# One block of sliding-window attention: the order of TensorE's products by array tile, and a mask product over 64 rows

## The chip, the cores and the metric

The kernel runs on one core of one Trainium2 chip. Its time is the device time of one execution in microseconds (us). The profile names the engines PE (TensorE's matmuls), PEld (TensorE's weight loads), DVE (VectorE), ACT (ScalarE), POOL (GpSimd) and SP (SyncE).

## The reference, cut to what matters

Two deformable convolutions on 8 images of 64 channels and 32x32 pixels come first. Then each image is 1024 tokens of 64 channels, and goes through sliding-window attention (8 heads, each query sees the 32 last keys) and a layer of experts. The change touches the attention alone:

```
q = (x @ Wq.T).reshape(b, t, h, e) / scale
kk = (xp @ Wk.T).reshape(b, tp, h, e) / scale
v = (xp @ Wv.T).reshape(b, tp, h, e)
idx = jnp.arange(t)[:, None] + jnp.arange(k)[None, :]
kw = kk[:, idx]
vw = v[:, idx]
dot = jnp.einsum('bthe,btkhe->bthk', q, kw)
attn = jax.nn.softmax(dot, axis=-1)
out = jnp.einsum('bthk,btkhe->bthe', attn, vw)
out = out.reshape(b, t, h * e)
return out @ Wu.T + bu
```

## The kernel before, in words

The attention works on blocks of 128 tokens of a pair of images: 32 blocks (ALL_BLOCKS). One image of the pair lies in partitions 0 to 63, the other in 64 to 127. Each engine has its own program, written out by hand, and the engines meet through counting semaphores; nothing else sets the order. Each program has a short lead-in, then a loop over 7 rounds of 4 blocks (`body(i)`, `BODY = 4`), and the last 4 blocks written out. Inside round b of the body several blocks are in flight: queries of block b+4, scores of b+3, keys of b+2, turned probabilities of b+1, values of b.

TensorE does these for a block, each product in float32 (two MATMUL records for one product) but for the mask:

- queries (L821): 8 products of 64 rows by 128 columns of the array, 128 columns of data each, the two images in the two halves of the rows. ScalarE copies the results out (L950).
- scores: first the mask, 2 products in float16 of 32 rows by 128 columns with 512 columns of data (L834), which write the mask into both score banks, then 16 products of 64 rows by 128 columns with 64 columns of data (L844). VectorE takes the maximum (L1007) and subtracts it (L1009, semaphore `shifted`), ScalarE takes the exponential (L956), VectorE sums (L1015) and inverts (L1017), GpSimd multiplies (L1085, `probs_ready`).
- turned probabilities (L869): 4 transposes of 128x128 for each image half ("image" 0 and 1), copied out by ScalarE (L962, `pt_ready`).
- turned keys (L857): 2 transposes of 128x128, copied out by VectorE (L1023, `xw_ready`).
- values (L888): 8 products of 64 rows by 64 columns for image 0, and 8 for image 1. ScalarE copies each result out (L968, `z_ready`).
- projection (L903): 8 products of 128 rows by 64 columns; VectorE adds the result to the tokens (L1033, `added`).

Ahead of the values of an image stand three waits (`before_values`). VectorE has raised `z_ready` to 1 before the first block, and every copy L968 adds 1:

```
pe.wait_ge(at.pt_ready, (i * BODY + b) * 2 + image + 1)
if image == 0:
    pe.wait_ge(at.xw_ready, i * BODY + b + 1)
pe.wait_ge(at.z_ready, (i * BODY + b) * 2 + image + 1)
```

So the values of image 1 of block b wait for a count of 2b + 2: 1 from VectorE, 2b copies of earlier blocks, and the copy of image 0 of block b itself.

TensorE's order in a round is queries (b+4), values of image 0 (b), turn of image 0 (b+1), mask and scores (b+3), values of image 1 (b), turn of image 1 (b+1), turned keys (b+2), projection (b). In two places the waits before the values stand one product early (`carry`), ahead of the last product of the queries and of the scores.

Of the kernel before, what the change touches and what calls it, by code (L numbers as in the profile page):

```python
# [15 lines left out]
NIMG, C, H, W = 8, 64, 32, 32  # L16
PAIRS = NIMG // 2
P = 128
# [655 lines left out]
HG = 2  # L674
H4 = HEADS // HG
# [120 lines left out]

TURN_AHEAD, KEYS_AHEAD, SCORES_AHEAD, QUERIES_AHEAD = 1, 2, 3, 4
ALL_BLOCKS = PAIRS * BLOCKS
# [11 lines left out]
def attention_pe(nc, pe, m, at):  # L810
    def queries(i, b, carry=None):

        pe.wait_ge(at.windows_ready, i * BODY + b + 1)
        if b:
            pe.wait_ge(at.g_ready, (i * BODY + b) * 2)
        for h in range(H4):
            for image in range(2):
                rows = slice(C * image, C * image + C)
                if carry is not None and (h, image) == (H4 - 1, 1):
                    carry()  # L820
                last = nc.tensor.matmul(m.ps[:, image, h * P:(h + 1) * P], at.a_heads[rows, h, :],  # L821
                                        at.window[rows, b % 4, WINDOW:SPAN], start=True, stop=True)
                if h == H4 - 1:
                    last.then_inc(at.g_in_psum, 1)

    def scores(i, b, carry=None):

        pe.wait_ge(at.g_ready, (i * BODY + b) * 2 + 2)
        pe.wait_ge(at.swapped_ready, (i * BODY + b) * 2 + 2)
        if b:  # L830
            pe.wait_ge(at.shifted, i * BODY + b)
        for hg in range(HG):
            rows = slice(TQ * hg, TQ * hg + TQ)
            nc.tensor.matmul(m.ps[:, 2 + hg, :], m.spread_q[rows, :], m.mask[rows, :], start=True, stop=False,  # L834
                             skip_group_check=True)
        for image in range(2):
            for j in range(TILES):
                first = (image * TILES + j % 2 * 2 + j // 2) * KEYS
                for hg in range(HG):
                    rows = slice(C * hg, C * hg + C)  # L840
                    keys = at.window if image == hg else at.swapped
                    if carry is not None and (image, j, hg) == (1, TILES - 1, HG - 1):
                        carry()
                    last = nc.tensor.matmul(m.ps[:, 2 + hg, first:first + KEYS], at.g[rows, b % 2, image, j, :],  # L844
                                            keys[rows, b % 4, j * TQ:j * TQ + KEYS], start=False, stop=True,
                                            skip_group_check=True)
        last.then_inc(at.scores_in_psum, 1)
# [25 lines left out]
    def before_values(i, b, image):  # L873

        pe.wait_ge(at.pt_ready, (i * BODY + b) * 2 + image + 1)
        if image == 0:
            pe.wait_ge(at.xw_ready, i * BODY + b + 1)
        pe.wait_ge(at.z_ready, (i * BODY + b) * 2 + image + 1)

    def values(b, image):  # L880
# [13 lines left out]
    def project_values(i, b):  # L894
        pe.wait_ge(at.z_ready, (i * BODY + b) * 2 + 3)
        if not exists(i, b + KEYS_AHEAD):

            pe.wait_ge(at.added, i * BODY + b + 2)
            pe.wait_ge(at.xw_ready, ALL_BLOCKS)
# [8 lines left out]
    def body(i):  # L908
        for b in range(BODY):
            if exists(i, b + QUERIES_AHEAD):  # L910
                queries(i, b + QUERIES_AHEAD, lambda: before_values(i, b, 0))
            else:
                before_values(i, b, 0)
            values(b, 0)
            if exists(i, b + TURN_AHEAD):
                turn_probs(i, b + TURN_AHEAD, 0)
            if exists(i, b + SCORES_AHEAD):
                scores(i, b + SCORES_AHEAD, lambda: before_values(i, b, 1))
            else:
                before_values(i, b, 1)  # L920
            values(b, 1)
            if exists(i, b + TURN_AHEAD):
                turn_probs(i, b + TURN_AHEAD, 1)
            if exists(i, b + KEYS_AHEAD):
                turn_keys(i, b + KEYS_AHEAD)
            project_values(i, b)

# [16 lines left out]
def attention_act(nc, act, m, at):  # L944
# [26 lines left out]
    def body(i):  # L971
        for b in range(BODY):
            if exists(i, b + QUERIES_AHEAD):
                queries(i, b + QUERIES_AHEAD)
            values(i, b, 0)
            if exists(i, b + TURN_AHEAD):
                probs(i, b + TURN_AHEAD, 0)
            values(i, b, 1)
            if exists(i, b + TURN_AHEAD):
                probs(i, b + TURN_AHEAD, 1)  # L980
            if exists(i, b + SCORES_AHEAD):
                exponentials(i, b + SCORES_AHEAD)

# [5 lines left out]
    exponentials(0, 1)  # L989
    exponentials(0, 2)  # L990
    for image in range(2):
# [291 lines left out]
def program(nc, a, out):  # L1283
    ctx = ExitStack()
    with ctx:
# [179 lines left out]
        at.projected = sem("at_projected")  # L1465
        at.added = sem("at_added")
        at.windows_ready = sem("at_windows_ready")
        at.swapped_ready = sem("at_swapped_ready")
# [308 lines left out]
def constants():  # L1777
# [19 lines left out]
    c["identity"] = np.eye(P, dtype=f32)  # L1797
    c["spread_q"] = np.tile(np.eye(TQ) * MASK_SCALE, (P // TQ, P // TQ)).astype(f16)

# [61 lines left out]
```

## Time and profile before

| | |
|---|---|
| median of 3 runs | 759.24 us (752.0 to 760.38) |
| the profiled execution | 755.67 us |
| its span, first to last instruction | 753.8 us |
| attention loop and last blocks, first values to last projection | 467.45 to 679.1 us of the span |

In the profile, a row of the timeline has the start in us from the span's start, the time in us, the engine, the line, the operation, what it writes and reads with the shape, how many were merged into the row, and in brackets how long the engine was idle before it and who released it. `64*128` before a shape is the piece of the array used, rows by columns. The end of a matmul is modelled; its start is not. The names of the buffers are those of the memory they share: `banks` are all PSUM banks, `src` holds the keys' windows, `s` the query weights, `y` the probabilities, the queries' results and the projection's weights, `hy` the turned keys, the turned probabilities and the values' results.

### The profile page before, as it was taken

The page shows a single profiled execution, that of the slowest core. Times are in us where ns is not written, and L with a number is a line of the kernel's source. Part 1 is how long each engine was busy: PE and PEld are TensorE (multiplying, and loading weights), DVE is VectorE, ACT ScalarE, POOL GpSimd, SP SyncE. Part 2 cuts the span into 40 slices and gives each one's busy share as a digit, 9 for nine tenths or more (in the row PEclk, how much of TensorE's full clock was granted, in tenths as well). Part 3 has the DMA queues.
Part 4 walks back from the last instruction along what each step waited for, and adds up shares of the span by engine and source line. Part 5 has one row for each costly group of instructions (what it writes and reads, how often), then busy time and mean ns, then how long its engine had stood idle before and what let it go on. Part 6 is the DMA issues. An engine that isn't in the chain of part 4 may idle for free.

```text
span 753.8 us, 32560 instructions
## 1 busy us (share of the span) xinstructions
PE 637.5 (85%) x14954; PEld 474.7 (63%) x14954; DVE 466.5 (62%) x560; ACT 369.4 (49%) x568; POOL 292.9 (39%) x287
## 2 busy tenths in 40 slices
PE   6479998898894898988887687999999999984475
PEld 1156666666742576766666576888888888863253
DVE  0587867788516876777763514766666676648523
ACT  0264555566423655556542433656655665553520
POOL 4045555566301654545540323344344434322200
PEclk9856899999996588999988555999999999997758
DMA  8310000000004000000001710000000000000002
GB/s 300 79 27 3 5 3 5 4 4 4 5 6 92 3 4 3 4 4 5 4 4 30 176 52 1 2 1 0 0 0 0 0 0 0 0 2 0 1 2 116
DMA packets 6403, 18.01 MB, mean 24 GB/s; under 512 B 1869, under 2 KB 4237, under 8 KB 5573
## 3 DMA queue, kind: packets, MB, share of 16 engines
q1 hardware_dynamic: 6286, 16.24, 7.8%
q8 instruction: 99, 1.62, 0.9%
q14 instruction: 18, 0.15, 0.1%
HBM read 12.37 MB, written 3.87 MB: 22 GB/s over the span
## 4 chain that ended last, share of the span: by engine, by line
PE 75%; DVE 7%; ACT 6%; DMA 4%; issue 4%; POOL 1%; SPq 1%; DVEq 0%; ACTq 0%
PE banks L268 21%; PE banks L199 11%; PE banks L844 9%; PE banks L821 5%; PE banks L888 5%; PE banks L869 5%; PE banks L903 4%; PE banks L171 3%; PE banks L185 2%; DMA off<-in_places_dram 2%; ACT y L301 2%; PE banks L834 1%; DMA off<-offsets_dram 1%; PE banks L229 1%; PE banks L615 1%
## 5 line engine op out<-in xcount | busy, mean ns | idle before, releaser
L322 POOL TENSOR_TENSOR y<-hy,hx 128x576 f32<-128x576 f32 (+1 forms) x104 | 167.5, 1633 | 200.4 <-DVE hy L396 197.3
L268 PE MATMUL banks<-y,xt 32*64 32x144 f32 (+1 forms) x6656 | 167.8, 306 | 25.0 <-issue 14.0
L268 PEld LDWEIGHTS banks<-y,xt 32*64 32x64 f32 x6656 | 114.7, 145 | 56.1 <-issue 36.8
L322 DVE TENSOR_TENSOR y<-hy,hx 128x576 f32<-128x576 f32 (+1 forms) x104 | 121.8, 1215 | 5.0 <-DVE hy L396 0.5
L1085 POOL TENSOR_TENSOR y<-y,stats 128x1024 f32<-128x1024 f32 x32 | 60.9, 1902 | 109.1 <-DVE stats L1017 109.0
L349 ACT ACTIVATE hx<-banks 128x768 f32<-128x768 f32 x96 | 62.1, 652 | 61.4 <-PE banks L171 58.6
L354 ACT ACTIVATE hy<-banks 128x768 f32<-128x768 f32 (+1 forms) x92 | 71.8, 805 | 38.5 <-PE banks L185 38.0
L301 DVE COPY y<-banks 128x768 f32<-128x768 f32 x48 | 45.8, 955 | 68.0 <-PE banks L268 68.0
L199 PE MATMUL banks<-y,w_dc 64*64 64x128 f32 x2304 | 84.7, 301 | 2.5 <-issue 1.2
L1007 DVE TENSOR_REDUCE stats<-banks 128x16 f32<-128x1024 f32 x32 | 39.2, 1225 | 69.3 <-PE banks L844 69.3
L199 PEld LDWEIGHTS banks<-y,w_dc 64*64 64x64 f32 x2304 | 75.4, 151 | 9.4 <-issue 7.1
L844 PEld LDWEIGHTS banks<-src,y 64*128 64x128 f32 x1024 | 64.5, 201 | 7.9 <-issue 7.9
L844 PE MATMUL banks<-src,y 64*128 64x64 f32 x1024 | 69.1, 289 | 0.0
L968 ACT COPY hy<-banks 128x512 f32<-128x512 f32 x64 | 38.0, 594 | 62.5 <-PE banks L888 62.5
L396 DVE TENSOR_SCALAR hy<-hy 128x1632 f32<-128x1632 f32 (+2 forms) x48 | 45.7, 953 | 10.1 <-ACT hy L354 10.1
L956 ACT ACTIVATE y<-y 128x1024 f32<-128x1024 f32 x32 | 33.9, 1059 | 27.1 <-DVE y L1009 27.0
L1015 DVE TENSOR_REDUCE stats<-y 128x16 f32<-128x1024 f32 x32 | 39.0, 1217 | 12.9 <-ACT y L956 12.9
L869 PE MATMUL banks<-identity,y 128*128 128x128 f32 x256 | 42.9, 291 | 3.1 <-ACT hy L962 3.1
L301 ACT COPY y<-banks 128x768 f32<-128x768 f32 x48 | 38.2, 796 | 14.1 <-PE banks L268 14.1
L888 PE MATMUL banks<-hy 64*64 64x128 f32 x1024 | 42.7, 282 | 1.8 <-ACT hy L968 1.8
L393 DVE TENSOR_SCALAR hx<-hx 128x1152 f32<-128x1152 f32 x48 | 39.0, 813 | 8.3 <-ACT hx L349 8.3
L821 PE MATMUL banks<-src,s 64*128 64x128 f32 x512 | 41.7, 308 | 1.7 <-ACT src L745 1.1
(141 smaller groups left out, 820.0 us busy)
## 6 DMA issues: line engine op xcount, KB each, us to landing
src<-in_x_dram SPq DMA_DIRECT2D x4, 578.0 KB, 5.6
y<-in_w_dram SPq DMA_DIRECT2D x1, 2080.0 KB
xt<-in_xt_dram SPq DMA_DIRECT2D x1, 2048.0 KB, 11.4
off<-in_w_dram SPq DMA_DIRECT2D x2, 1024.0 KB
out_dram<-tokens SPq DMA_DIRECT2D x4, 512.0 KB, 3.8
offsets_dram<-tokens SPq DMA_DIRECT2D x32, 54.0 KB
off<-offsets_dram SPq DMA_DIRECT2D x16, 108.0 KB
w_dc<-in_w_dc_dram SPq DMA_DIRECT2D x2, 288.0 KB, 9.2
```

The lines of the kernel that those rows point to most:

```text
L199: last = nc.tensor.matmul(m.ps[C * g:C * g + C, bank + p // 2, 0:PLACES], cv.w_dc[rows, tap, :], m.sampled[rows, row % 2, p, tap, :], star ...
L268: last = nc.tensor.matmul(ap(out, [[UNIT_ROWS * PITCH - 2, 3], [PITCH, strip.n], [1, WIN_COLS]]), m.xt[32 * j:32 * j + 32, strip.tile_row, ...
L301: return copy(ap(m.sampled[:, unit.row % 2, j, 3 * unit.ky, :], [[TAPS * PLACES, 2], [W, 3 * UNIT_ROWS], [1, W]]), ap(m.ps[:, j, 4:], [[BA ...
L322: multiply(dst, hy, hx, ALU.mult).then_inc(cv.s_ready[g], 1)
L349: nc.scalar.activation(m.hx[:, u % 2, :, first:end], m.ps[:, bank:bank + 2, 0:end - first], ACT.Abs).then_inc(cv.emptied, 1)
L354: nc.scalar.activation(ap(m.hy[:, u % 2, 0, strips[0].at * HAT_ROW:], [[Y_HATS, 2], [HAT_PITCH, 3 * n_rows], [1, W]]), ap(m.ps[:, bank, :] ...
L396: nc.vector.tensor_scalar(hat, hat, 1.0, 1.0, ALU.min, ALU.subtract).then_inc(cv.hats, 1)
L821: last = nc.tensor.matmul(m.ps[:, image, h * P:(h + 1) * P], at.a_heads[rows, h, :], at.window[rows, b % 4, WINDOW:SPAN], start=True, stop ...
L844: last = nc.tensor.matmul(m.ps[:, 2 + hg, first:first + KEYS], at.g[rows, b % 2, image, j, :], keys[rows, b % 4, j * TQ:j * TQ + KEYS], st ...
L869: last = nc.tensor.transpose(m.ps[:, 4, k * P:(k + 1) * P], at.p[:, b % SLOTS_P, hg, image, odd, :], m.identity[:, :])
L888: last = nc.tensor.matmul(m.ps[C * hg:C * hg + C, 5 + late, first:first + P], at.xw[rows, b % 2, odd, C * image:C * image + C], at.pt[rows ...
L1085: nc.gpsimd.tensor_tensor(p, p, scale.unsqueeze(2).to_broadcast([P, 2 * TILES * HG, KEYS]), ALU.mult).then_inc(at.probs_ready, 1)
```

## The change

The order of TensorE in a round becomes: values of image 0 and of image 1 (b), turn of image 0 (b+1), queries (b+4), mask and scores (b+3), projection (b), turn of image 1 (b+1), turned keys (b+2). The `carry` places go away. The mask product reads 64 rows instead of 32, of which the added 32 hold zeros in `spread_q`. The projection waits for the sum of the block before (`added`) and for a copy of turned keys (`xw_ready`) in every block. A semaphore `values_begun` is raised before the values of each image; no engine waits for it. ScalarE's order in a round becomes: both copies of values (b), exponential, copy of turned image 0 (b+1), two copies of queries (b+4), copy of turned image 1 (b+1), and the exponential is that of block b+2 instead of b+3, so that one of the three exponentials of the lead-in moves into the loop. VectorE's and GpSimd's programs stay as they are.

```diff
-TURN_AHEAD, KEYS_AHEAD, SCORES_AHEAD, QUERIES_AHEAD = 1, 2, 3, 4
+TURN_AHEAD, KEYS_AHEAD, EXPS_AHEAD, SCORES_AHEAD, QUERIES_AHEAD = 1, 2, 2, 3, 4
...
         for hg in range(HG):
-            rows = slice(TQ * hg, TQ * hg + TQ)
+            rows = slice(C * hg, C * hg + C)
             nc.tensor.matmul(m.ps[:, 2 + hg, :], m.spread_q[rows, :], m.mask[rows, :], start=True, stop=False,
...
         pe.wait_ge(at.z_ready, (i * BODY + b) * 2 + image + 1)
+        pe.sem_inc(at.values_begun, 1)
...
         pe.wait_ge(at.z_ready, (i * BODY + b) * 2 + 3)
-        if not exists(i, b + KEYS_AHEAD):
-
-            pe.wait_ge(at.added, i * BODY + b + 2)
+        pe.wait_ge(at.added, i * BODY + b + 2)
+        if exists(i, b + KEYS_AHEAD):
+            pe.wait_ge(at.xw_ready, i * BODY + b + 2)
+        else:
             pe.wait_ge(at.xw_ready, ALL_BLOCKS)
...
     def body(i):
         for b in range(BODY):
-            if exists(i, b + QUERIES_AHEAD):
-                queries(i, b + QUERIES_AHEAD, lambda: before_values(i, b, 0))
-            else:
-                before_values(i, b, 0)
-            values(b, 0)
+            for image in range(2):
+                before_values(i, b, image)
+                values(b, image)
             if exists(i, b + TURN_AHEAD):
                 turn_probs(i, b + TURN_AHEAD, 0)
+            if exists(i, b + QUERIES_AHEAD):
+                queries(i, b + QUERIES_AHEAD)
             if exists(i, b + SCORES_AHEAD):
-                scores(i, b + SCORES_AHEAD, lambda: before_values(i, b, 1))
-            else:
-                before_values(i, b, 1)
-            values(b, 1)
+                scores(i, b + SCORES_AHEAD)
+            project_values(i, b)
             if exists(i, b + TURN_AHEAD):
                 turn_probs(i, b + TURN_AHEAD, 1)
             if exists(i, b + KEYS_AHEAD):
                 turn_keys(i, b + KEYS_AHEAD)
-            project_values(i, b)
...
     def body(i):
         for b in range(BODY):
+            for image in range(2):
+                values(i, b, image)
+            if exists(i, b + EXPS_AHEAD):
+                exponentials(i, b + EXPS_AHEAD)
+            if exists(i, b + TURN_AHEAD):
+                probs(i, b + TURN_AHEAD, 0)
             if exists(i, b + QUERIES_AHEAD):
                 queries(i, b + QUERIES_AHEAD)
-            values(i, b, 0)
-            if exists(i, b + TURN_AHEAD):
-                probs(i, b + TURN_AHEAD, 0)
-            values(i, b, 1)
             if exists(i, b + TURN_AHEAD):
                 probs(i, b + TURN_AHEAD, 1)
-            if exists(i, b + SCORES_AHEAD):
-                exponentials(i, b + SCORES_AHEAD)
...
-    exponentials(0, 2)
...
-    c["spread_q"] = np.tile(np.eye(TQ) * MASK_SCALE, (P // TQ, P // TQ)).astype(f16)
+    spread = np.concatenate([np.eye(TQ) * MASK_SCALE, np.zeros((C - TQ, TQ))])
+    c["spread_q"] = np.tile(spread, (P // C, P // TQ)).astype(f16)
```

TensorE's queue in one round of the loop before, from the last product of the queries to the values of image 1 (L821 queries, L888 values, L869 turned probabilities, L834 mask, L844 scores):

```order
L821 MATMUL banks<-src,s 128x128 [waits at_z_ready,at_xw_ready,at_pt_ready]
L888 MATMUL banks<-hy 64x128 x8
L869 MATMUL banks<-identity,y 128x128 [waits at_pt_ready,at_probs_ready]
L869 MATMUL banks<-identity,y 128x128 x3
L828 REGISTER_ALU
L834 MATMUL banks<-mask,spread_q 128x512 [waits at_shifted,at_swapped_ready,at_g_ready]
L834 MATMUL banks<-mask,spread_q 128x512
L844 MATMUL banks<-src,y 128x64 x15
L875 REGISTER_ALU
L844 MATMUL banks<-src,y 128x64 [waits at_z_ready,at_pt_ready]
L888 MATMUL banks<-hy 64x128 x8
```

The round after, from the values of image 0 to the mask (L885 values, L865 turned probabilities, L819 queries, L832 mask; the scores L840, the projection L901, the turn of image 1 and the turned keys L853 follow):

```order
L885 MATMUL banks<-hy 64x128 [waits at_z_ready,at_pt_ready,at_xw_ready]
L885 MATMUL banks<-hy 64x128 x7
L885 MATMUL banks<-hy 64x128 [waits at_pt_ready,at_z_ready]
L885 MATMUL banks<-hy 64x128 x7
L865 MATMUL banks<-identity,y 128x128 [waits at_pt_ready,at_probs_ready]
L865 MATMUL banks<-identity,y 128x128 x3
L813 REGISTER_ALU
L815 REGISTER_ALU [waits at_windows_ready]
L819 MATMUL banks<-src,s 128x128 [waits at_g_ready]
L819 MATMUL banks<-src,s 128x128 x7
L826 REGISTER_ALU
L832 MATMUL banks<-mask,spread_q 128x512 [waits at_shifted,at_swapped_ready,at_g_ready]
```

The two lots of values now stand next to each other, and the second still carries its wait for `z_ready`; before, the turn, the mask and the scores stood between them.

ScalarE's queue in the loop before (L950 queries' copies, L968 values' copies, L962 turned probabilities' copies, L956 exponential):

```order
L949 ISA [waits at_scores_in_psum]
L950 COPY y<-banks 128x4x4x32 [waits at_g_in_psum]
L949 REGISTER_ALU
L950 COPY y<-banks 128x4x4x32 [waits at_g_in_psum]
L966 REGISTER_ALU
L968 COPY hy<-banks 128x512 [waits at_z_in_psum,at_projected]
L961 ISA [waits at_z_in_psum]
L962 COPY hy<-banks 128x512 [waits at_pt_in_psum]
L968 COPY hy<-banks 128x512 [waits at_z_in_psum]
L961 REGISTER_ALU [waits at_z_in_psum]
L962 COPY hy<-banks 128x512 [waits at_pt_in_psum]
L956 ACTIVATE y<-y 128x1024 [waits at_shifted]
```

After (L963 values' copies, L951 exponential, L957 turned probabilities' copies, L945 queries' copies):

```order
L963 COPY hy<-banks 128x512 [waits at_z_in_psum,at_projected]
L963 COPY hy<-banks 128x512 [waits at_z_in_psum]
L951 ACTIVATE y<-y 128x1024 [waits at_shifted]
L956 ISA [waits at_z_in_psum]
L957 COPY hy<-banks 128x512 [waits at_pt_in_psum]
L944 ISA [waits at_scores_in_psum]
L945 COPY y<-banks 128x4x4x32 [waits at_g_in_psum]
L944 REGISTER_ALU
L945 COPY y<-banks 128x4x4x32 [waits at_g_in_psum]
L956 REGISTER_ALU [waits at_z_in_psum]
L957 COPY hy<-banks 128x512 [waits at_pt_in_psum]
```

The copy of the first lot of values has nothing ahead of it but the copy of turned image 1 of the round before, and the exponential stands behind both copies of values.

## Rows read from the trace of the kernel before

**Rows 1.** The page: busy time and share of the span, and the chain that ended last.

```profile
PE 637.5 (85%) x14954; PEld 474.7 (63%) x14954; DVE 466.5 (62%) x560; ACT 369.4 (49%) x568; POOL 292.9 (39%) x287
...
PE 75%; DVE 7%; ACT 6%; DMA 4%; issue 4%; POOL 1%; SPq 1%; DVEq 0%; ACTq 0%
```

**Rows 2.** Windows: loop, last blocks, lead-in; columns as in the first line.

```profile
core 0: us, PE busy (x) PEld busy (x) DVE busy (x) ACT busy (x) POOL busy (x), PEclk, DMA share, GB/s
467.45:655.22 187.77, 187.77 (x2919) 153.55 (x2917) 122.49 (x160) 113.00 (x189) 76.11 (x105) 1.00 0.00 0
655.22:679.15 23.93, 21.36 (x348) 16.52 (x346) 11.72 (x17) 13.21 (x23) 5.71 (x3) 1.00 0.01 2
440.00:467.45 27.45, 23.20 (x176) 19.65 (x176) 11.84 (x14) 8.73 (x13) 5.70 (x9) 0.50 0.00 1
```

**Rows 3.** Timeline of PE, one round of the loop.

```profile
566.33 2.00 PE L844 MATMUL banks<-src,y 64*128 64x64 f32 x32
568.26 0.67 PE L888 MATMUL banks<-hy 64*64 64x128 f32 x16
568.86 0.66 PE L869 MATMUL banks<-identity,y 128*128 128x128 f32 x4
569.35 0.38 PE L857 MATMUL banks<-identity,src 128*128 128x128 f32 x2
569.66 1.09 PE L903 MATMUL banks<-hy,y 128*64 128x128 f32 x16
570.68 1.16 PE L821 MATMUL banks<-src,s 64*128 64x128 f32 x16
571.78 0.67 PE L888 MATMUL banks<-hy 64*64 64x128 f32 x16
572.38 0.66 PE L869 MATMUL banks<-identity,y 128*128 128x128 f32 x4
572.96 0.39 PE L834 MATMUL banks<-mask,spread_q 32*128 32x512 f16 x2
573.28 2.00 PE L844 MATMUL banks<-src,y 64*128 64x64 f32 x32
```

**Rows 4.** Line L869, 470 to 655 us: ns min/median/max of its records.

```profile
L869 PE MATMUL banks<-identity,y x212: 272/273/328, 471.5 to 652.7; 128*128 128x128 f32 x106
```

**Rows 5.** Timeline of all engines, the last two blocks.

```profile
671.25 0.67 PE L888 MATMUL banks<-hy 64*64 64x128 f32 x16
...
672.77 0.67 PE L888 MATMUL banks<-hy 64*64 64x128 f32 x16 [0.27 <-ACT hy L968]
...
675.16 0.67 PE L888 MATMUL banks<-hy 64*64 64x128 f32 x16
...
675.95 0.59 ACT L968 COPY hy<-banks 128x512 f32<-128x512 f32 x1 [1.25 <-PE banks L888]
...
676.68 0.67 PE L888 MATMUL banks<-hy 64*64 64x128 f32 x16 [0.85 <-ACT hy L968]
...
678.04 1.09 PE L903 MATMUL banks<-hy,y 128*64 128x128 f32 x16 [0.70 <-ACT hy L968]
```

**Rows 6.** Timeline of DVE, the same round of the loop.

```profile
568.38 1.23 DVE L1007 TENSOR_REDUCE stats<-banks 128x16 f32<-128x1024 f32 x1 [1.84 <-PE banks L844]
...
571.98 1.22 DVE L1015 TENSOR_REDUCE stats<-y 128x16 f32<-128x1024 f32 x1 [0.43 <-ACT y L956]
```

**Rows 7.** Timeline, the lead-in's end: PE, ACT and POOL.

```profile
462.81 1.06 ACT L956 ACTIVATE y<-y 128x1024 f32<-128x1024 f32 x1 [5.53 <-DVE y L1009]
...
464.34 1.90 POOL L1085 TENSOR_TENSOR y<-y,stats 128x1024 f32<-128x1024 f32 x1 [3.97 <-DVE stats L1017]
464.40 1.11 PE L869 MATMUL banks<-identity,y 128*128 128x128 f32 x4 [3.10 <-ACT hy L962]
...
465.44 2.08 PE L821 MATMUL banks<-src,s 64*128 64x128 f32 x16
```

**Rows 8.** A window over the last blocks, columns as in rows 2.

```profile
665.00:680.00 15.00, 11.73 (x193) 8.73 (x186) 5.78 (x11) 7.87 (x13) 2.77 (x2) 1.00 0.01 2
```

More of the change, by code:

```diff
@@ L810, in attention_pe, with queries @@
 def attention_pe(nc, pe, m, at):
-    def queries(i, b, carry=None):
+    def queries(i, b):
         pe.wait_ge(at.windows_ready, i * BODY + b + 1)
@@ L818, in queries @@
                 rows = slice(C * image, C * image + C)
-                if carry is not None and (h, image) == (H4 - 1, 1):
-                    carry()
                 last = nc.tensor.matmul(m.ps[:, image, h * P:(h + 1) * P], at.a_heads[rows, h, :],
@@ L824, in queries, with scores @@
                     last.then_inc(at.g_in_psum, 1)
-    def scores(i, b, carry=None):
+    def scores(i, b):
         pe.wait_ge(at.g_ready, (i * BODY + b) * 2 + 2)
@@ L841, in scores @@
                     keys = at.window if image == hg else at.swapped
-                    if carry is not None and (image, j, hg) == (1, TILES - 1, HG - 1):
-                        carry()
                     last = nc.tensor.matmul(m.ps[:, 2 + hg, first:first + KEYS], at.g[rows, b % 2, image, j, :],
@@ L1466, in program @@
         at.added = sem("at_added")
+        at.values_begun = sem("at_values_begun")
         at.windows_ready = sem("at_windows_ready")
```

## The prediction

> **What bounds the kernel now.** I read the page first: TensorE is busy for 85% of the span and makes up 75% of the chain that ended last, with no other engine above 7% [rows 1]. Then the windows over the attention: from the first values to those of block 27 TensorE is never idle (187.77 us of 187.77) and its granted clock is 1.00, its level of 2.4 GHz; VectorE has 122.49 us of work in it, ScalarE 113.00, GpSimd 76.11 [rows 2]. These are 27 rounds, so a round takes 6.95 us, of which VectorE works 4.5 and ScalarE 4.2. So in the loop the time is TensorE's own sequence and nothing else. The reader is to see in the timeline how that sequence splits by starts: scores 1.93, values 0.60, turn 0.49, keys 0.31, projection 1.02, queries 1.10, values 0.60, turn 0.58, mask 0.32, which add up to 6.95 [rows 3].
>
> **What a change of array tile costs.** The same four transposes take 0.49 us up to the keys, which use the same 128x128 tile, and 0.58 up to the mask, which uses another [rows 3]: 0.09 us for what comes behind. The first of a group is modelled at 328 ns against 273 for the rest [rows 4], so some 0.05 more lies in front. One change costs about 0.14 us. Before there are eight in a round (values, turn, mask, scores, values, turn with keys, projection, queries). After there are five: values, turn, queries with mask and scores, projection, turn with keys.
>
> The Trainium skill (TensorEngine Tiling (Array Packing), Key Properties) says that a change of tiling mode drains TensorE. By that rule, a mask of 64 rows joins the queries and scores without a drain although it is float16 and they are float32; the trace shows no such neighbours. The sum would then be the one below, and with drains left on both sides of the mask that of the second rival.
>
> **Part 1, the merged stages.** From the rows, with 0.09 taken off behind and 0.05 in front where a change falls away: queries 1.10 becomes 1.01, mask 0.32 becomes 0.22, scores 1.93 becomes 1.88, and values of image 0 up to those of image 1 would take 0.50, then 0.55 up to the turn, in place of 0.60 twice. Turns 0.58 and 0.49, keys 0.31 and projection 1.02 stay. Sum: 0.50 + 0.55 + 0.58 + 1.01 + 0.22 + 1.88 + 1.02 + 0.49 + 0.31 = 6.56 us, a gain of 0.39 a round. That the mask reads 64 rows costs nothing by the rows' logic, since the time goes by its 512 columns; I bound it by 0 and by one more mask product, 0.2 us.
>
> **Part 2, the wait that comes to lie bare.** The values of image 1 wait until z_ready has counted 2b + 2, so until ScalarE has copied the values of image 0 of the same block. Before, turn, mask and scores lie between the two, 0.60 + 0.58 + 0.32 + 1.93 = 3.43 us from start to start [rows 3], and the copy is long done. Now nothing lies between. The trace has this very sequence once, in block 31, where there is nothing left to turn or to score: values at 675.16, copy at 675.95 for 0.59, values again at 676.68, with TensorE idle for 0.85 us [rows 5]. Start to start that is 1.52 us. In block 30 a turn lies between, and it is again 1.52 (671.25 to 672.77) [rows 5], so it is the copy that sets it and not TensorE's work. In place of 0.50 the step takes 1.52, which is 1.02 us a round. Behind the waiting product stand TensorE's whole queue, and so everybody. Nothing else is free to fill it. The turn, which could, now stands behind the second values.
>
> Can ScalarE be late for that copy? In the new order the piece ahead of it is the copy of turned image 1, whose turn ends with the keys and values of image 0 still to come (some 0.8 us of TensorE), so it is done about 0.2 us before the copy can start. The wait for pt_ready of image 1 is covered by the same stall. Cost 0, bound 0.1.
>
> **Part 3, the raised semaphore.** values_begun is one more instruction of TensorE's sequencer before each lot of values. No row shows one on TensorE; the nearest is the whole way from ScalarE's end to the next product, 676.54 to 676.68, 0.14 us [rows 5]. One of the two lies behind the stall and counts in full. I take 0.05 a round, bounds 0 and 0.14.
>
> **A round after:** 6.56 + 1.02 + 0.05 = 7.63, and the values behind a stall again have a slow first product, 0.05: 7.68 us, which is 0.73 more than before.
>
> **Part 4, the other queues.** ScalarE's exponential of block b+3 moves a round later. VectorE's sums of that block wait for it, and the maximum of the next block is queued behind them. Counted from the first values of a round: scores end at 5.9, maximum and subtraction (1.23 each [rows 6]) take VectorE to 8.4; the exponential comes at 3.9 of the next round, 11.6 in all, and sum and reciprocal, about 1.5 [rows 6], end at 13.1, while the next scores end at 13.6. So it fits, by 0.5 us. GpSimd's product is then due at 15.0 and needed at about 17.5. The projection's new waits are for work done a round earlier. All at 0; if VectorE's 0.5 us were used up, it would cost what exceeds it, and I keep 0.2 a round for the range.
>
> **Part 5, lead-in and end.** In the lead-in the copy of turned image 0 no longer stands behind the exponential that began at 462.81; TensorE was idle for 3.10 us before 464.40, so the turn before it had ended at 461.3, and with a copy of 0.6 in between TensorE's second turn starts at about 462.0 and not 464.40 [rows 7]. That gains 2.4 us, but the turn of block 1 then waits for GpSimd's product, which ends at 466.24 [rows 7], and the queries, at the lower clock level of 1.2 GHz there (2.0 us for what takes 1.1 in the loop [rows 3, 7]), come behind it. The first values of block 1 then start at 472.4 if the clock rises where it did, at 467.5, and near 477.4 if the round is at the low level throughout; before it was 474.4. That is -2 to +3 us; I take +0.5. For the end, before took 23.93 us from the values of block 27 on [rows 2]. After: 7.68, then 6.67 (no queries), about 5.5 (no scores; the turn of image 1 waits for a copy behind the last exponential), 4.6, and 4.0 for the last: 28.5, so +4.6.
>
> **The sum:** 26 rounds x 0.73 = 19.0, plus 4.6, plus 0.5: **+24 us**. Against the profiled execution's own 755.67 that is 780; against the median of 759.24, 783. The two differ by noise of the runs (752.0 to 760.38), and I state 781.
>
> **Rivals.**
> 1. **The copy is hidden after all, and the change gains.** This needs that the second lot of values doesn't wait for the copy of the first. The rounds then take 6.56 to 6.61: 26 x -0.37 = -10, with about +1 at the ends, so 747 to 750 us. The tile argument speaks for it. Against it speak the count of the semaphore, and block 31, in which the wait named is just this copy [rows 5]. It decides from a stall under 0.4 us a round. 4%. A middle case, a stall of about 0.4, would give no change: 3%.
> 2. **The change doesn't do what it says:** the mask still costs a drain on both sides, because its type differs. Then 0.28 a round come on top, over some 30 rounds: +8, 789 us. The trace can't tell, since before the mask differs from its neighbours in both tile and type [rows 3]. 12%.
> 3. **The clock falls.** TensorE would be idle for 0.9 us of 7.7, every round, and at 1.2 GHz a round takes roughly twice TensorE's 6.6 plus the stall, 14 us. Every round at that level costs 6 us more. Against it: from 665 to 680 us TensorE is idle for 3.3 of 15 us, in gaps of up to 0.85, and the granted clock stays 1.00 [rows 5, 8]. For it: in the lead-in the clock was 0.50 over 27 us with TensorE busy for 23.2 [rows 2], so it may also rise late, a round or two of 6 us. A steady low clock gives over 850 us. 6% for more than three such rounds.
>
> The Trainium skill (TensorE: Matmul & The Clock Gate, A second HAM failure mode) says that frequent short idling between groups of matmuls makes the clock swing between its levels. By it this third rival would be the likely one; rows 8 speak against it here.
>
> 4. **My forecast:** stall of 1.0 us a round and the clock as now, 772 to 792. 75%.
>
> **How the numbers follow.** Rival 2's time lies within my range's upper half. The low end is 752.0, the lowest run before, plus 19 (the best lead-in, no cost for the semaphore): 771. The high end adds to 783 two rounds at the low clock or the mask's drains with some of VectorE's 0.2: 798. Left out are the first rival, the middle case and most of the third. A measurement of this kernel tells about 1% from no change. Slower by over 1%: 75 + 12 + 6 = 93, less 1 for a mixed case: 92%; same 3%; faster 5%.
>
> **What the profile after would show.** Values in two groups of 16 records 1.5 to 1.65 us apart by start, with TensorE idle for 0.85 to 1.0 us in front of the second, put down to ScalarE's copy of values, some 31 times. Rounds of 7.6 to 7.8 us. Queries, mask and scores with 0.11 between their neighbours and not 0.2; if the mask is followed by scores 0.32 later, the second rival holds. The granted clock at 1.00 over the loop. It would be wrong if the second values started 0.5 us after the first, if the rounds differed in length (the clock), or if VectorE's maximum began later than the scores' end.

## The result and the profile after

The changed kernel takes 770.49 us (median of 4 runs, 766.85 to 770.95), the kernel before 757.38 us over its 4 runs; the ratio is 1.0178, with a 95% interval of 1.0113 to 1.0244. It is slower, as forecast, by 13 us and not by 24, and half a microsecond under the low end of the range (771). Ratios and their intervals, here and below, compare only executions in the faster of the two states that each kernel's executions fall into, while medians are over all, so that the medians don't give the ratio. The profiled execution took 766.85 us with a span of 765.0 us, so 11.2 us over the profiled one before.

The page answers to [rows 1]: TensorE has 14 us less of busy time, and a smaller share of the chain; ScalarE has a larger one.

```profile
PE 623.1 (81%) x14954; PEld 470.0 (61%) x14954; DVE 464.1 (61%) x560; ACT 368.7 (48%) x568; POOL 293.7 (38%) x287
...
PE 72%; ACT 8%; DVE 7%; issue 5%; DMA 4%; POOL 2%; SPq 1%; ACTq 0%; DVEq 0%; POOLq 0%
```

The windows of the kernel after: from the values of block 1 to those of block 27, then the end, then three pieces of the lead-in.

```profile
core 0: us, PE busy (x) PEld busy (x) DVE busy (x) ACT busy (x) POOL busy (x), PEclk, DMA share, GB/s
468.12:663.49 195.37, 174.72 (x2809) 148.98 (x2808) 117.29 (x157) 108.29 (x183) 74.14 (x104) 1.00 0.00 0
663.49:691.02 27.53, 22.25 (x363) 17.57 (x362) 12.72 (x20) 14.54 (x24) 5.71 (x3) 1.00 0.01 1
437.00:443.50 6.50, 5.87 (x46) 5.19 (x48) 0.42 (x1) 2.15 (x4) 1.11 (x4) 0.50 0.00 0
443.50:453.75 10.25, 7.33 (x118) 6.75 (x117) 6.61 (x7) 5.54 (x7) 0.00 (x0) 1.00 0.01 2
453.75:464.00 10.25, 8.16 (x71) 6.22 (x70) 4.57 (x5) 3.78 (x6) 5.58 (x8) 0.50 0.01 2
```

And the same stretches of the kernel before, cut at the values of blocks 0, 1 and 27:

```profile
436.91:467.45 30.54, 25.89 (x194) 21.73 (x194) 12.19 (x14) 9.71 (x14) 6.83 (x13) 0.50 0.00 1
467.45:474.43 6.98, 6.98 (x110) 5.71 (x109) 3.08 (x4) 4.08 (x7) 2.75 (x4) 0.99 0.01 2
474.43:655.22 180.79, 180.79 (x2811) 147.84 (x2809) 119.42 (x156) 108.92 (x183) 73.36 (x101) 1.00 0.00 0
```

26 rounds take 195.37 us instead of 180.79, that is 7.51 a round against 6.95, and TensorE, never idle before, is idle for 20.6 us of them (195.37 less 174.72), 0.79 a round. The granted clock is 1.00 throughout. One round of the timeline of PE shows where, and answers to [rows 3]:

```profile
565.81 0.67 PE L885 MATMUL banks<-hy 64*64 64x128 f32 x16
567.28 0.67 PE L885 MATMUL banks<-hy 64*64 64x128 f32 x16 [0.81 <-ACT hy L963]
567.88 0.66 PE L865 MATMUL banks<-identity,y 128*128 128x128 f32 x4
568.47 1.16 PE L819 MATMUL banks<-src,s 64*128 64x128 f32 x16
569.46 0.38 PE L832 MATMUL banks<-mask,spread_q 64*128 64x512 f16 x2
569.68 1.90 PE L840 MATMUL banks<-src,y 64*128 64x64 f32 x32
571.50 1.09 PE L901 MATMUL banks<-hy,y 128*64 128x128 f32 x16
572.53 0.66 PE L865 MATMUL banks<-identity,y 128*128 128x128 f32 x4
573.02 0.38 PE L853 MATMUL banks<-identity,src 128*128 128x128 f32 x2
573.33 0.67 PE L885 MATMUL banks<-hy 64*64 64x128 f32 x16
```

The one idle time stands in front of the second lot of values, and its releaser is ScalarE's copy of the first. By starts: values 1.47, then 0.60, turn 0.59, queries 0.99, mask 0.22, scores 1.82, projection 1.03, turn 0.49, keys 0.31, in all 7.52. The stages that now share a tile follow each other sooner: queries 0.99 (1.10 before), mask 0.22 (0.32), scores 1.82 (1.93).

ScalarE's timeline of the same round:

```profile
565.70 0.59 ACT L957 COPY hy<-banks 128x512 f32<-128x512 f32 x1 [2.22 <-PE banks L865]
566.60 0.59 ACT L963 COPY hy<-banks 128x512 f32<-128x512 f32 x1 [0.32 <-PE banks L885]
```

The copy of turned image 1 is over before the copy of values begins, and ScalarE even waits 0.32 us between them. From 565.81 to 566.60 it waits for the values to land, copies for 0.59, and 0.09 us after its end TensorE starts again.

### The profile page after: what moved, and what is told of

Its sections match the earlier page's. It is cut to its first block, busy times and chain, and to the rows that moved or that the text cites. A ratio compares the mean times of both kernels' runs of the same rounds, so it can differ in the third digit from the quotient of the medians.

```text
span 765.0 us, 32615 instructions
## 1 busy us (share of the span) xinstructions
PE 623.1 (81%) x14954; PEld 470.0 (61%) x14954; DVE 464.1 (61%) x560; ACT 368.7 (48%) x568; POOL 293.7 (38%) x287
## 4 chain that ended last, share of the span: by engine, by line
PE 72%; ACT 8%; DVE 7%; issue 5%; DMA 4%; POOL 2%; SPq 1%; ACTq 0%; DVEq 0%; POOLq 0%
PE banks L268 20%; PE banks L199 11%; PE banks L840 7%; PE banks L885 5%; PE banks L865 5%; PE banks L819 5%; PE banks L901 4%; PE banks L171 3%; ACT hy L963 3%; PE banks L185 2%; DMA off<-in_places_dram 2%; ACT y L301 2%; DMA off<-offsets_dram 1%; PE banks L229 1%; PE banks L615 1%
## 5 line engine op out<-in xcount | busy, mean ns | idle before, releaser
L268 PE MATMUL banks<-y,xt 32*64 32x144 f32 (+1 forms) x6656 | 165.1, 304 | 25.8 <-issue 15.0
L268 PEld LDWEIGHTS banks<-y,xt 32*64 32x64 f32 x6656 | 113.1, 144 | 56.4 <-issue 37.5
L957 ACT COPY hy<-banks 128x512 f32<-128x512 f32 x64 | 37.2, 582 | 72.0 <-PE banks L865 72.0
L885 PE MATMUL banks<-hy 64*64 64x128 f32 x1024 | 43.6, 286 | 25.4 <-ACT hy L963 25.4
L840 PEld LDWEIGHTS banks<-src,y 64*128 64x128 f32 x1024 | 63.6, 191 | 1.0
L840 PE MATMUL banks<-src,y 64*128 64x64 f32 x1024 | 61.8, 271 | 0.0
L963 ACT COPY hy<-banks 128x512 f32<-128x512 f32 x64 | 37.5, 586 | 36.0 <-PE banks L885 35.9
L885 PEld LDWEIGHTS banks<-hy 64*64 64x64 f32 x1024 | 28.8, 135 | 37.9 <-issue 37.9
L865 PE MATMUL banks<-identity,y 128*128 128x128 f32 x256 | 43.4, 293 | 1.8 <-ACT hy L957 1.0
## 6 DMA issues: line engine op xcount, KB each, us to landing
xt<-in_xt_dram SPq DMA_DIRECT2D x1, 2048.0 KB, 11.2
```

The lines of the kernel that those rows point to most:

```text
L268: last = nc.tensor.matmul(ap(out, [[UNIT_ROWS * PITCH - 2, 3], [PITCH, strip.n], [1, WIN_COLS]]), m.xt[32 * j:32 * j + 32, strip.tile_row, ...
L865: last = nc.tensor.transpose(m.ps[:, 4, k * P:(k + 1) * P], at.p[:, b % SLOTS_P, hg, image, odd, :], m.identity[:, :])
L885: last = nc.tensor.matmul(m.ps[C * hg:C * hg + C, 5 + late, first:first + P], at.xw[rows, b % 2, odd, C * image:C * image + C], at.pt[rows ...
L963: nc.scalar.copy(at.z[:, image, :].rearrange("p (a n) -> p a n", a=2), m.ps[:, 5:7, image * 2 * P:(image + 1) * 2 * P]).then_inc(at.z_read ...
```

## The experiments

Rounds below are the distance of the first values of blocks 1 and 27, divided by 26. The kernel before was measured anew beside each group of experiments, and each median belongs beside the one of its group: 758.80 us for mask64_only, mask32_in_new_order, turn_between and image1_other_banks; 757.85 for banks_turn_early, values_apart, inc_in_before and exp_three_ahead; 758.38 for mask64_again, before_again and after_again.

**mask64_only**: the kernel before, with the mask product alone changed.

```diff
-            rows = slice(TQ * hg, TQ * hg + TQ)
+            rows = slice(C * hg, C * hg + C)
...
+    spread = np.concatenate([np.eye(TQ) * MASK_SCALE, np.zeros((C - TQ, TQ))])
+    c["spread_q"] = np.tile(spread, (P // C, P // TQ)).astype(f16)
```

> The kernel before with the mask product over 64 rows and nothing else. Theory A (what costs is a change of the piece of the array, some 0.14 us each, and float16 beside float32 costs nothing): the change between mask and scores goes away, a round takes 6.80 to 6.83 us instead of 6.95, mask to scores 0.22 and scores 1.88, time 4 to 5 us under the kernel before. Rival B (the type of the mask sets the drain): a round stays at 6.95 and the time the same.

Rounds of 6.75 us, so 0.20 less and not 0.12 to 0.15. Its timeline of PE:

```profile
569.69 0.39 PE L834 MATMUL banks<-mask,spread_q 64*128 64x512 f16 x2
569.91 1.90 PE L844 MATMUL banks<-src,y 64*128 64x64 f32 x32
571.74 0.67 PE L888 MATMUL banks<-hy 64*64 64x128 f32 x16
```

Mask to scores 0.22 (0.32 in [rows 3]), scores 1.83 (1.93). Rival B falls, and beside float32 scores of the same tile the float16 mask shows no cost for its type: its step is the 0.22 us that Part 1 had for a mask with no change behind it. This change of tile is worth 0.20 us: 0.10 behind the mask and 0.10 in front of the scores, of which I had seen only 0.05. The median was 743.69 us, 15 under the kernel before, more than 31 rounds of 0.20 can give.

**mask64_again**: the same kernel.

> mask64_only once more, unchanged. Its rounds save 0.20 us each, 6 us in all, but its median lay 15 us under the kernel before. If the other 9 us were noise of the stretches outside the attention, the ratio is now 0.985 to 0.995; if the mask does something outside the loop as well, 0.98 again.

751.96 us, 6.4 less than the kernel before by the medians; ratio 0.9854 (0.9811 to 0.9898), which is 8 to 14 us less; rounds again 6.75. The products that the mask touches give about 7 us: 0.20 in each of 29 rounds, and 1.0 in the lead-in (below, at Part 5). That fits the medians, but lies just under what the ratio allows, and what the remainder is isn't shown. The stretches outside the attention (the span less what lies from the first queries to the start of the last projection's last product) took 505 us in the first profile of this kernel and 515 in the second, with the same instructions, so differences as large as what is left over of the 15 us do arise there.

**mask32_in_new_order**: the changed kernel with the mask product put back to 32 rows.

> The changed kernel with the mask product back at 32 rows. Theory A: two changes of tile come back around the mask, 0.25 to 0.30 us a round, rounds of 7.75 to 7.80 us instead of 7.51, time 8 us over the changed kernel, so 778. Rival B: no difference in the rounds, 770.

784.31 us, ratio 1.0449 (1.0357 to 1.0540); rounds of 7.84 us, 0.33 over the changed kernel's, for two changes of tile. Its timeline of PE has them on both sides of the mask:

```profile
568.00 1.16 PE L819 MATMUL banks<-src,s 64*128 64x128 f32 x16
569.10 0.39 PE L832 MATMUL banks<-mask,spread_q 32*128 32x512 f16 x2
569.42 2.00 PE L840 MATMUL banks<-src,y 64*128 64x64 f32 x32
571.35 1.09 PE L901 MATMUL banks<-hy,y 128*64 128x128 f32 x16
```

1.10, 0.32 and 1.93, as in [rows 3], against 0.99, 0.22 and 1.82 in the changed kernel. The change between mask and scores is the one that mask64_only takes away, 0.20 us; the one between queries and mask is then worth the other 0.12. Without the wider mask a round of the new order would be 0.89 us longer than before and not 0.56. The time came out 6 us above the 778 that I expected: in this profile the lead-in (first queries to the values of block 1) took 40.0 us at a clock of 0.50, where the changed kernel's took 31.1.

**turn_between**: the changed kernel with the turn of image 0 between the two lots of values.

```diff
-            for image in range(2):
-                before_values(i, b, image)
-                values(b, image)
+            before_values(i, b, 0)
+            values(b, 0)
             if exists(i, b + TURN_AHEAD):
                 turn_probs(i, b + TURN_AHEAD, 0)
+            before_values(i, b, 1)
+            values(b, 1)
```

> The changed kernel with the turn of image 0 put between the two lots of values. Theory A (ScalarE's copy sets the distance of the two lots, whatever lies between): still 1.47 us from first to second values, the idle time falls from 0.81 to about 0.3, rounds of 6.9 to 7.0 us (0.59 of the turn hidden, less two changes of tile that are in the shadow of the wait), time 754 to 758. Rival D (the restart after a stall, or the lost head start of TensorE's sequencer, costs and not the copy itself): the distance grows by the turn to 2.0, rounds stay near 7.5, 770 us.

755.74 us, ratio 1.0019 (0.9965 to 1.0073), rounds of 6.93 us. From its timeline of PE:

```profile
569.87 0.67 PE L885 MATMUL banks<-hy 64*64 64x128 f32 x16
570.47 0.66 PE L865 MATMUL banks<-identity,y 128*128 128x128 f32 x4
571.29 0.67 PE L885 MATMUL banks<-hy 64*64 64x128 f32 x16 [0.17 <-issue]
571.89 1.16 PE L819 MATMUL banks<-src,s 64*128 64x128 f32 x16
```

The second values begin 1.42 us after the first (1.47 in three rounds of four; 1.42 comes in the first block of each turn of the loop, in the changed kernel too), with or without a turn between. What sets the distance is the chain from the first values through ScalarE's copy of them, and 0.59 us of work put into it is 0.59 us saved. Rival D falls.

**image1_other_banks**: the wait taken away, and with it the sharing of banks that it stands for. Both lots of values are written to banks 5 and 6, at different columns, and the wait keeps TensorE from writing there while ScalarE copies out the first lot. Here image 1 goes to the queries' banks, and the scores come before the queries.

```diff
-        pe.wait_ge(at.z_ready, (i * BODY + b) * 2 + image + 1)
+        if image:
+            if exists(i, b + QUERIES_AHEAD):
+                pe.wait_ge(at.g_ready, (i * BODY + b + QUERIES_AHEAD) * 2)
...
+        pe.wait_ge(at.z_ready, (i * BODY + b) * 2 + 1)
...
-                    last = nc.tensor.matmul(m.ps[C * hg:C * hg + C, 5 + late, first:first + P],
+                    last = nc.tensor.matmul(m.ps[C * hg:C * hg + C, (0 if image else 5) + late, first:first + P],
```

(ScalarE's copy reads image 1 from those banks, and the queries wait until it has; these lines and the swap of scores and queries are left out here.)

> The changed kernel with the values of image 1 in the banks of the queries (0 and 1), so that they needn't wait for the copy of image 0; the mask and scores come before the queries. Theory A (the only loss is the bare wait for the copy of the first lot of values): first to second values 0.5 to 0.65 us by start, rounds of 6.55 to 6.7 us, time 741 to 750 us, faster than both kernels. Rival C (another wait of the new order takes its place, ScalarE's copy of turned image 1 or VectorE's sums behind the later exponential): first to second values still 1 us or more, or TensorE idle elsewhere, rounds of 6.95 or more and 757 us or more.

739.54 us, ratio 0.9856 (0.9782 to 0.9931), rounds of 6.74 us. The two lots now lie 0.71 to 0.77 us apart. A round is 0.77 us shorter than the changed kernel's 7.51. But rounds came out above my 6.55 to 6.7: as rival C had it, only smaller, another wait had taken the place of the first. From the timeline of all engines:

```profile
571.47 0.66 PE L867 MATMUL banks<-identity,y 128*128 128x128 f32 x4
...
572.22 0.58 ACT L964 COPY hy<-banks 128x512 f32<-128x512 f32 x1 [0.60 <-PE banks L867]
572.27 0.42 PEld L892 LDWEIGHTS banks<-hy 64*64 64x64 f32 x16 [0.17 <-issue]
...
573.02 0.46 PEld L892 LDWEIGHTS banks<-hy 64*64 64x64 f32 x16 [0.32 <-issue]
```

The copy of turned image 1 ends at 572.80, and the weights of the second values load from 573.02 on. PE shows no idle time there, because the ends of its products are modelled; the distance of the two lots shows the wait.

**banks_turn_early**: image1_other_banks with the projection moved behind the turn of image 1 and the turned keys.

```diff
-            project_values(i, b)
             if exists(i, b + TURN_AHEAD):
                 turn_probs(i, b + TURN_AHEAD, 1)
             if exists(i, b + KEYS_AHEAD):
                 turn_keys(i, b + KEYS_AHEAD)
+            project_values(i, b)
```

> The kernel image1_other_banks (values of image 1 in the queries' banks) with the turn of image 1 and the turned keys ahead of the projection. Theory A (in image1_other_banks the 0.25 us left between the two lots was the copy of turned image 1, which began only when that turn had ended): the projection now hides that copy, first to second values 0.5 us, rounds of 6.45 to 6.55 us, time 5 to 9 us under image1_other_banks. Rival C (VectorE's sums behind the later exponential hold the next scores): rounds stay near 6.74.

731.63 us, ratio 0.9700 (0.9639 to 0.9760), the fastest of all, 3% under the kernel before. Rounds of 6.45 us, and TensorE is never idle in them:

```profile
464.19:631.89 167.70, 167.70 (x2811) 146.25 (x2809) 114.89 (x156) 105.77 (x182) 72.16 (x103) 1.00 0.00 0
```

The two lots begin 0.49 us apart in every round, so theory A holds for the second wait too. The changed kernel's round of 7.51 us thus has about 1.06 us of bare waiting in it. With five changes of tile and nothing bare, a round is 0.50 us shorter than before, for three changes fewer: 0.17 each on average.

**values_apart**: the kernel before with the mask over 64 rows (the lines of mask64_only) and the queries moved next to it; the values stay apart.

```diff
-            if exists(i, b + QUERIES_AHEAD):
-                queries(i, b + QUERIES_AHEAD, lambda: before_values(i, b, 0))
-            else:
-                before_values(i, b, 0)
+            before_values(i, b, 0)
             values(b, 0)
             if exists(i, b + TURN_AHEAD):
                 turn_probs(i, b + TURN_AHEAD, 0)
+            if exists(i, b + QUERIES_AHEAD):
+                queries(i, b + QUERIES_AHEAD)
```

(ScalarE's copies of the queries move likewise, and values_begun is raised.)

> The kernel before with the mask over 64 rows and the queries moved next to mask and scores, values of image 1 still behind the scores: six changes of tile in a round and nothing bare. A change of tile is worth 0.20 us by mask64_only: rounds of 6.55 to 6.65 us. If it is 0.14: 6.65 to 6.7. If the queries' copies come too late for ScalarE: TensorE idle in front of the values of image 1, rounds over 6.75. Time 5 to 15 us under the kernel before.

745.07 us, ratio 0.9849 (0.9774 to 0.9924), rounds of 6.65 us, 0.30 less than before for two changes of tile fewer. Against mask64_only (6.75) the second of them is worth only 0.10, and from here to banks_turn_early (6.45) the third is worth 0.20; so a change has no single price here, and what decides it isn't shown. Of the 0.50 us that banks_turn_early gains in a round, 0.30 need no new banks, only that the two lots don't become neighbours.

**inc_in_before**: the kernel before with one line more.

```diff
         pe.wait_ge(at.z_ready, (i * BODY + b) * 2 + image + 1)
+        pe.sem_inc(at.values_begun, 1)
```

> The kernel before with values_begun raised before each lot of values, and nothing else. If the raised semaphore costs what the prediction took, where nothing is bare: rounds of 6.95 to 7.05, in the last two blocks first to second values 1.57 instead of 1.52. The rival, from the trace after (1.47 from first to second values in block 31, where before had 1.52): it is cheaper than nothing, 1.47 in the last two blocks, rounds 6.95.

757.13 us, ratio 0.9980 (0.9929 to 1.0032), rounds of 6.95. Its last block, from the timeline of PE:

```profile
680.77 0.67 PE L889 MATMUL banks<-hy 64*64 64x128 f32 x16
682.25 0.67 PE L889 MATMUL banks<-hy 64*64 64x128 f32 x16 [0.81 <-issue]
```

1.48 us and 0.81 idle, where [rows 5] have 1.52 and 0.85. Raising the semaphore costs nothing in the loop and makes the release after a wait 0.05 us shorter: all four profiles without it have 1.52 in block 31. Why is not shown.

**exp_three_ahead**: the changed kernel with the exponential again that of block b+3, at the end of ScalarE's round.

```diff
-            if exists(i, b + EXPS_AHEAD):
-                exponentials(i, b + EXPS_AHEAD)
...
+            if exists(i, b + EXPS_AHEAD):
+                exponentials(i, b + EXPS_AHEAD)
```

> The changed kernel with ScalarE's exponential again that of block b+3, at the round's end, and three of them in the lead-in. The theory that the wait for the copy is the loss says that whatever stands ahead of the copy in ScalarE's queue adds to it: the exponential waits for VectorE until 0.8 us into the round, so the copy of the first values starts at 1.9 instead of 0.8, first to second values about 2.5 us, rounds of 8.4 to 8.7 us, time 25 to 33 us over the changed kernel. The rival (the exponential has room elsewhere): rounds of 7.5. In the lead-in the first values start 2.4 us later than in the changed kernel at the same clock.

841.97 us, ratio 1.1159 (1.1084 to 1.1234), some 71 us over the changed kernel where I had expected 25 to 33. The distance of the two lots is 2.43 us and a round at the full clock 8.49, both as expected. From the timelines of PE and ACT:

```profile
526.31 0.67 PE L885 MATMUL banks<-hy 64*64 64x128 f32 x16
528.74 0.67 PE L885 MATMUL banks<-hy 64*64 64x128 f32 x16 [1.77 <-ACT hy L963]
529.34 1.12 PE L865 MATMUL banks<-identity,y 128*128 128x128 f32 x4
```

```profile
527.11 1.06 ACT L951 ACTIVATE y<-y 128x1024 f32<-128x1024 f32 x1 [0.33 <-DVE y L1004]
528.08 0.57 ACT L963 COPY hy<-banks 128x512 f32<-128x512 f32 x1
```

But the turn behind that wait takes 1.12 us instead of 0.66, with the granted clock at 0.50 from 529.4 to 530.3, and the mean round is 9.98 us. Over the loop:

```profile
467.28:726.72 259.44, 215.44 (x2810) 184.19 (x2809) 117.45 (x157) 113.16 (x183) 74.11 (x104) 0.83 0.00 0
```

The third rival of the prediction, then, does happen, but at an idle time of 1.77 us in a round of 8.5 and not at 0.81 in 7.5. So moving the exponential was what kept the change from being much worse.

**before_again** and **after_again**: both kernels once more.

> The kernel before once more, unchanged, to see how far two programs that are the same lie apart: ratio 1.00 within 1%, rounds 6.95. Its profile gives a second sample of the lead-in (first queries to the values of block 1: 37.5 us in the first profile) and of all that lies outside the attention (511.8 us). If these stretches move with the clock alone, they come out different by several us though the instructions are the same.

761.05 us, ratio 0.9949 (0.9895 to 1.0003); rounds of 6.95. From the first queries to the values of block 1 its profile takes 41.9 us (37.5 the first time), and outside the attention 514.0 (511.8). In the lead-in the cause is the clock: it was at 0.50 for the 40.3 us to the end of this window, and in the first profile for 30.5 us.

```profile
439.49:479.80 40.31, 35.66 (x280) 29.62 (x282) 14.63 (x16) 13.84 (x21) 9.33 (x16) 0.50 0.00 1
```

> The changed kernel once more, unchanged. Rounds 7.51 as before. If the short lead-in of its first profile (31.1 us to the values of block 1) came from the clock being at its upper level for 10 us in it, a profile without that stretch has 35 to 37 us there, as turn_between and values_apart have. Ratio to the kernel before 1.012 to 1.025.

770.71 us, ratio 1.0136 (1.0092 to 1.0180); rounds of 7.51, and the lead-in again 31.09 us. The window shows the same stretch at the full clock:

```profile
442.14:448.60 6.46, 5.83 (x46) 5.14 (x47) 0.42 (x1) 2.12 (x4) 1.10 (x4) 0.50 0.00 0
448.60:458.80 10.20, 7.28 (x116) 6.69 (x116) 6.60 (x7) 5.57 (x8) 0.00 (x0) 1.00 0.01 2
```

I had also allowed for a profile of this kernel without that stretch; none is on record.

## Why the prediction was wrong in size and right in kind

The direction, the mechanism and its place were right: the wait for z_ready lies bare, once a round, released by ScalarE's copy, with the clock at 1.00. image1_other_banks and turn_between show that what lies bare is the wait for this copy. What failed is sizes: the lead-in of Part 5, put at +0.5 us, measured -6.4, and the round, put at 0.73 us more, measured 0.56 more. The low end of the range was 771; the miss is by 0.5 us, and it took both errors, since either alone would have left the result inside (781 less 6.9 is 774, less 4.4 is 777). The profiled executions differ by 11.2 us, where my sum had 24.1:

| term | predicted | measured |
|---|---|---|
| 26 rounds | 19.0 (0.73 each) | 14.6 (0.56 each) |
| from the values of block 27 to the end | +4.6 | +3.6 |
| first queries to the values of block 1 | +0.5 (-2 to +3) | -6.4 |
| all else | 0 | -0.6 |

The end is 1.0 us less than forecast, 0.4 of it in the round of block 29 (5.08 us for my 5.5).

**The rounds, Part 2 and Part 3.** I took 1.52 us for first to second values from [rows 5] and added 0.05 for the raised semaphore. It measured 1.47, and 1.42 in one round of four. inc_in_before shows that the instruction makes the release shorter: its sign was wrong, and my bounds (0 and 0.14) left a gain out. This is 0.10 to 0.15 of the 0.17 us a round.

**The tiles, Part 1 and the worth of a change.** 0.14 us was too little where the mask meets the scores: the row of the scores went from 2.00 to 1.90, so 0.10 lies in front and not 0.05, and the scores' step is 1.82 and not 1.88. The queries and the mask held: predicted 1.01 and 0.22, measured 0.99 and 0.22. Together with the last point that makes the 0.17. That all changes cost the same was wrong too, as far as the pairs above go: 0.20 between mask and scores, 0.12 between queries and mask.

**Part 4, the other queues.** Held. VectorE's maximum waits 0.53 us for the scores (I had 0.5 of room), from the timeline of DVE after:

```profile
571.62 1.23 DVE L1001 TENSOR_REDUCE stats<-banks 128x16 f32<-128x1024 f32 x1 [0.53 <-PE banks L840]
```

**Part 5, the lead-in.** The largest single error. Three things are in it. The exponential moved out of it gave the 2.4 us that I had: turn_between, without it, needs 25.08 us from the first queries to the first values, values_apart, with it, 27.49, both at the lower clock level all the way. The windows of turn_between, values_apart and mask64_only:

```profile
429.97:455.05 25.08, 22.88 (x178) 20.25 (x179) 9.72 (x11) 8.18 (x12) 3.92 (x8) 0.50 0.00 1
429.71:457.20 27.49, 22.87 (x178) 20.24 (x178) 12.07 (x14) 9.12 (x13) 5.00 (x9) 0.50 0.00 1
430.03:459.53 29.50, 24.89 (x195) 22.03 (x195) 12.19 (x14) 9.71 (x14) 6.80 (x13) 0.50 0.00 1
```

The wider mask gives 1.0 us, which I hadn't counted: mask64_only takes 29.50 us for this stretch and the kernel before 30.54, both at 0.50, with three pairs of mask products in it.

The third is the clock. The changed kernel needs only 21.61 (437.00 to 458.61), 3.5 less than turn_between, because its clock was at 1.00 for 10 us there (its windows above), while before had 0.50 throughout. turn_between has the same instructions in that stretch and not that clock, so they alone don't decide it. Both profiles of the changed kernel have such a stretch, and so have those of image1_other_banks, banks_turn_early and exp_three_ahead; mask32_in_new_order and turn_between don't, nor does any kernel of the old order. I looked for a late rise only behind the lead-in and took for granted that inside it the clock would be as in before; my bound of -2 lacked these 3.5 us and the mask's 1.0. What makes the clock rise there stays open.

**The rivals.** The copy is not hidden (the first rival); the mask's type costs nothing that shows (the second falls by mask64_only); the clock didn't fall in the changed kernel (the third), though it did in exp_three_ahead, with twice the idle time. The Trainium skill (TensorEngine Tiling (Array Packing), Key Properties) says that a change of tiling mode drains TensorE; the runs agree in that each change taken away made a round 0.10 to 0.20 us shorter, and mask64_only shows no such cost where only the type changes. The Trainium skill (TensorE: Matmul & The Clock Gate, A second HAM failure mode) says that frequent short idling between groups of matmuls makes the clock swing; exp_three_ahead agrees (clock 0.83 over the loop), the changed kernel doesn't (1.00).

## What to carry to other kernels

Before two stages are made neighbours to save a change of the array's tile, look at what waits between them: a change is 0.10 to 0.20 us here, a bare wait for a copy out of a shared PSUM bank 0.81 to 1.0 us. The stages that stand between two others cost changes of tile and cover the wait at once, so price both before moving them, and if the stages must meet, give them banks of their own and look which wait comes next; here that turned a loss of 1.8% (1.4% when measured again) into a gain of 3%. The last block, written out behind the loop, showed the price beforehand, because there the covering stages had run out. In a lead-in at a low clock, the clock belongs in the range with several microseconds to either side: here it gave 3.5 us to the changed kernel, and took 4.4 from the kernel before in its second profile.

## What the runs showed of the hardware that was not expected

- A change of the array's tile cost 0.20 us between float16 mask and float32 scores when both sides are counted (rounds of 6.95 and 6.75 us), 0.12 between float32 queries and the mask (7.84 and 7.51, less the 0.20), and 0.17 on average over the three that banks_turn_early saves (6.95 and 6.45).
- A raised semaphore ahead of waiting products made TensorE's restart 0.05 us faster (1.47 or 1.48 us from first to second values against 1.52) and cost nothing where nothing waits (6.95 us a round with and without).
- The granted clock stayed at 1.00 with TensorE idle for 0.81 us in rounds of 7.5 us, and swung, with a mean of 0.83 over the loop, with 1.77 us idle in rounds of 8.5 us at the full clock.
- The same instructions took 21.6 and 25.1 us in the lead-in, the first with 10 us at a granted clock of 1.00, the second at 0.50 throughout. Outside the attention the same instructions took 505 and 515 us in the two profiles of mask64_only's kernel, whose mean granted clock was 0.867 and 0.868 over the span; why is not shown.
